# Test-time memory scan of a four-layer transformer: where VectorE forms the second activation and the second scores of a chunk

## What is computed

```python
def step(carry, xs):                       # for every token
    Sm = et * Sm - tt * gt                 # momentum of the gradient
    Wm = (1.0 - at) * Wm + Sm              # memory weights W1, W2 (32x32 each)
    return ((Sm, Wm), Wm)
for c0 in range(0, S, CHUNK):              # CHUNK = 64 tokens
    g = grad(|silu(k W1^T) W2^T - v|^2) at the W of the chunk's start, * 0.1
    g = g * min(1 / max(|g|, 1e-6), 1)     # clipped by its norm, per token
    (S_state, W_state), Wtraj = scan(step, (S_state, W_state), g)
    h = silu(q W1t^T)                      # read-out with the W of each token
    outs.append(h W2t^T)
```

## Time and profile before

| | |
|---|---|
| median of 3 runs | 3209.58 us (3208.36 to 3209.92) |
| profiled execution | 3204.99 us |
| its span | 3203.2 us |
| busy: TensorE, VectorE, ScalarE, GpSimd | 2956.0, 2241.2, 1444.0, 734.6 us |
| the scan (first `hd` to last `retr`) | 2798.90 to 2986.27 us |
| TensorE matmul / VectorE / GpSimd busy from 2799.00 to 2986.30 | 167.04 / 112.60 / 102.36 us |

### The profile page before, as it was taken

The page is one execution under the profiler, slowest core; times in us unless marked ns, Lnnn a source line. Parts: engine busy times, 40 slices in busy tenths (PEclk is TensorE's granted clock), DMA queues, the critical chain, the costliest instruction groups (busy, mean ns, idle before and its releaser), DMA issues. The chain is left out here.

```text
span 3203.2 us, 43118 instructions
## 1 busy us (share of the span) xinstructions
PE 2956.0 (92%) x15784; PEld 1831.3 (57%) x15784; DVE 2241.2 (70%) x4554; ACT 1444.0 (45%) x2691; POOL 734.6 (23%) x608
## 2 busy tenths in 40 slices
PE   5999999999986999999999999999998666789699
PEld 3666666666653555555555555555554342455487
DVE  5788888888616877777777877777764567766554
ACT  2666666666621444444444444444444310322243
POOL 1000000000000344444444444444443000055100
PEclk7999999999976999999999999999999857555598
DMA  4112212120005101111111101111100000000000
GB/s 95 26 32 44 50 26 51 30 46 21 1 8 119 22 19 40 40 40 40 40 40 27 40 19 35 40 40 40 40 1 31 6 7 3 1 1 1 17 1 14
DMA packets 40336, 95.81 MB, mean 30 GB/s; under 512 B 12296, under 2 KB 29374, under 8 KB 30398
## 3 DMA queue, kind: packets, MB, share of 16 engines
q1 hardware_dynamic: 40126, 93.06, 12.9%
HBM read 35.10 MB, written 7.34 MB: 13 GB/s over the span
## 5 line engine op out<-in xcount | busy, mean ns | idle before, releaser
L916 ACT ACTIVATE l1a_PT<-l1a_st 128x512 f32<-128x512 f32 x1024 | 596.5, 598 | 759.8 <-PE l1a_st L832 755.9
L933 DVE TENSOR_REDUCE l1a_m<-l1a_aux 128x1 f32<-128x512 f32 x1024 | 667.7, 685 | 124.9 <-PE l1a_aux L794 123.0
L441 DVE TENSOR_REDUCE l0s_mquad<-l0s_mx 128x1 f32<-128x512 f32 x1024 | 635.6, 684 | 169.6 <-PE l0s_mx L309 169.6
L883 POOL TENSOR_TENSOR l1a_acc<-l1a_acc,l1a_PT 128x1024 f32<-128x1024 f32 x224 | 569.7, 2543 | 680.5 <-ACT l1a_PT L916 680.5
L417 ACT ACTIVATE l0s_PT<-l0s_st 128x512 f32<-128x512 f32 x1024 | 528.6, 602 | 237.0 <-PE l0s_st L325 234.4
L845 PE MATMUL l1a_ov<-l1a_PT,l1a_V 128*64 128x512 f32 x2048 | 495.7, 605 | 0.0
L830 PE MATMUL l1a_st<-l1a_QA,l1a_KA 128*128 128x512 f32 x1024 | 446.9, 436 | 2.3 <-issue 2.3
L325 PE MATMUL l0s_st<-l_QS,l_KS 128*128 128x512 f32 x1024 | 438.1, 431 | 3.7 <-ACT l0s_PT L417 3.6
L309 PE MATMUL l0s_mx<-l_KS,l_QS 120*128 120x512 f32 x1024 | 415.6, 413 | 20.4 <-DMA l_KS<-qk_rows 20.4
L832 PE MATMUL l1a_st<-l1a_QB,l1a_KB 65*128 65x512 f32 x1024 | 405.3, 396 | 0.0
L794 PE MATMUL l1a_aux<-l1a_KA,l1a_QA 128*128 128x512 f32 x1024 | 398.5, 437 | 0.8 <-DVE l1a_lo L945 0.8
(11 more groups left out here) (352 smaller groups left out, 2844.4 us busy)
## 6 DMA issues: line engine op xcount, KB each, us to landing
l1a_KA<-l1a_hi SPq DMA_DIRECT2D x32, 512.0 KB, 8.1
l_QS<-qk_rows SPq DMA_DIRECT2D x64, 192.0 KB
l_KS<-qk_rows SPq DMA_DIRECT2D x64, 192.0 KB
l1a_QA<-l1a_hi SPq DMA_DIRECT2D x16, 512.0 KB, 4.6
l1a_QA<-l1a_lo SPq DMA_DIRECT2D x16, 512.0 KB, 8.7
l1a_QB<-l1a_hi SPq DMA_DIRECT2D x16, 512.0 KB, 4.6
l1a_KB<-l1a_lo SPq DMA_DIRECT2D x16, 512.0 KB, 6.5
qk_rows<-l0s_hi SPq DMA_DIRECT2D x64, 64.0 KB, 6.8
```

What stands on the lines that cost most here:

```text
L441: nc.vector.tensor_reduce(mquad[:, u % 2, tile, g:g + 1], mx[:, n % MX0, :], axis=AX.X, op=ALU.max).then_inc(mx_free[n % MX0], 1)
L883: nc.gpsimd.tensor_tensor(acc[:, h % 2, 1, :], first, PT[:, g % PT_SLOTS, :], ALU.add).then_inc(added_pool, 1)
L916: nc.scalar.activation(PT[:, g % PT_SLOTS, (u % 2) * CW:(u % 2 + 1) * CW], st[:, u % ST1, :], ACT.Exp, scale=1.0 / float(np.sqrt(HD1))).th ...
L933: nc.vector.tensor_reduce(m4[:, b, q, c:c + 1], src, axis=AX.X, op=ALU.max).then_inc(aux_read, 1)
```

## The change

The read-out moves one chunk nearer on all engines. On VectorE `h2` of chunk c-1 no longer stands between the state writes but behind `side`, ahead of `gn`. `m2` is now of chunk c-1, not c-2, and stands behind the `dwe` pair, ahead of the state write. TensorE does `hh` of c-1 and `y2` of c-2 in iteration c, GpSimd `h2a` and `h2c` of c-1, ScalarE `retr` of c-2, so that each of these loops has one iteration less behind the last chunk. Buffers and instructions are the same in number. The last chunk's `h2` and `m2` follow behind VectorE's loop.

```diff
-            for c in range(NCH + 3):
+            for c in range(NCH + 2):
...
-                if 0 <= c - 2 < NCH:
-                    o = c - 2
+                if 0 <= c - 1 < NCH:
+                    o = c - 1
                     pe.wait_ge(s["h2_ready"], o + 1)
...
                     nc.tensor.matmul(hh, hd[:, o % 3, :], h2[:, :], start=True, stop=True).then_inc(s["hh_full"], 1)
-                if 0 <= c - 3:
-                    o = c - 3
+                if 0 <= c - 2:
+                    o = c - 2
                     pe.wait_ge(s["h2s_ready"], 2 * (o + 1))
                     pe.wait_ge(s["m2_ready"], o + 1)
...
-                if c >= 2:
-                    o = c - 2
+                if c >= 1:
+                    o = c - 1
                     pool.wait_ge(s["h2_ready"], o + 1)
...
+                link(nc.vector.tensor_scalar(side[:, :], pn, hn[:, :], EPS3 ** 2 / NORM_SCALE, ALU.mult, ALU.max))
+                if c >= 1:
+                    second_activation(c - 1)
+                dve.wait_ge(s["zn_full"], c + 1)
...
+                    nc.vector.scalar_tensor_tensor(dwe[:, c % 4, i, :], root.broadcast_to([CHUNK, DM]), 1.0 / COEF_UNIT,
+                                                   grad, op0=ALU.min, op1=ALU.mult).then_inc(s[done], 1)
+                if c >= 1:
+                    second_scores(c - 1)
+                new = (c + 1) % 4
+                dve.wait_ge(s["first_full"], c + 1)
...
+            second_activation(NCH - 1)
+            second_scores(NCH - 1)
```

More of the change, by code:

```diff
@@ L2005, in _ @@
                         pe.wait_ge(s["tok_done"], 3 * c)
-                    if c >= 3:
-                        pe.wait_ge(s["m2_ready"], c - 2)
+                    if c >= 2:
+                        pe.wait_ge(s["m2_ready"], c - 1)
                     nc.tensor.transpose(htok, hd[:, c % 3, :], ident[0:DM, 0:DM]).then_inc(s["htok_full"], 1)
@@ L2011, in _ @@
                         pe.wait_ge(s["w2_done"], c)
-                    if c >= 4:
-                        pe.wait_ge(s["y2_read"], c - 3)
+                    if c >= 3:
+                        pe.wait_ge(s["y2_read"], c - 2)
                     nc.tensor.matmul(dh, W2[:, c % 2, :], dp[:, :], start=True, stop=True).then_inc(s["dh_full"], 1)
@@ L2070, in _ @@
                         nc.scalar.activation(tok[:, i, :], htok, ACT.Copy, scale=half[:, i, c:c + 1]).then_inc(s["tok_done"], 1)
-                if 0 <= c - 3:
-                    act.wait_ge(s["y2_full"], c - 2)
-                    nc.scalar.activation(T["retr"][:, at(c - 3)], y2, ACT.Copy).then_inc(s["y2_read"], 1)
+                if 0 <= c - 2:
+                    act.wait_ge(s["y2_full"], c - 1)
+                    nc.scalar.activation(T["retr"][:, at(c - 2)], y2, ACT.Copy).then_inc(s["y2_read"], 1)
         @block.gpsimd
@@ L2078, in _ @@
             pool.wait_ge(s["consts_done"], 1)
-            for c in range(NCH + 2):
+            for c in range(NCH + 1):
                 if c < NCH:
@@ new lines, in second_activation, with second_scores @@
+            def second_activation(o):
+                dve.wait_ge(s["e2_done"], o + 1)
+                if o >= 1:
+                    dve.wait_ge(s["hh_full"], o)
+                    dve.wait_ge(s["h2s_ready"], 2 * o)
+                nc.vector.scalar_tensor_tensor(h2[:, :], e2[:, :], 1.0, y1, op0=ALU.add, op1=ALU.mult
+                                               ).then_inc(s["h2_ready"], 1)
+            def second_scores(o):
+                dve.wait_ge(s["hh_full"], o + 1)
+                if o >= 1:
+                    dve.wait_ge(s["y2_full"], o)
+                nc.vector.scalar_tensor_tensor(m2[:, :], hh, thM[:, o:o + 1], T["C"][0:CHUNK, at(o)],
+                                               op0=ALU.mult, op1=ALU.mult).then_inc(s["m2_ready"], 1)
```

115 lines of the change are left out of this document (46 added, 69 removed).

## The result

The changed kernel takes 3195.41 us (median of 5 runs, 3189.05 to 3198.23) beside 3209.58 us (5 runs, 3204.42 to 3212.07): ratio 0.9957, 95% interval 0.9944 to 0.9970. That is 13.8 us less by the ratio (9.6 to 18.0 by its interval), 14.2 between the medians. The forecast was 11.6 less, 3198.0 us. The direction and the mechanism came as forecast. The profiled execution took 3189.05 us.

A forecast was written before the change was run, and what follows sets the result against it. The scan was taken as a loop of latencies, 5.66 us between state writes, with no engine full. Savings of 9.0 + 2.6 = 11.6 us, all other parts 0, took 3209.6 to 3198.0 us; range 3195.5 to 3203.0.

The forecast's parts named there:

- The gap ahead of `y1`: TensorE between `z` and `pred`: `y1` no longer waits for `h2`, saving 0.32 us in 28 chunks, 9.0 us.
- The end: Behind the last chunk: the last `hh` starts at about 2980.35 instead of 2982.91, saving 2.6 us.
- `h2` in its new place: VectorE between `side` and `gn`: `h2` fits before `gn` starts, cost 0; up to 0.21 a chunk without cover.
- `gn` still idle ahead of it, about 0.1: Sign of a right forecast on VectorE: idle time ahead of `gn` of about 0.1 in place of 0.31 us.
- `hh` behind it: TensorE: `hh` following the moved `h2` starts 0 to 0.09 us later, cost 0.
- `m2` ahead of the state write: VectorE behind the `dwe` pair: `m2` is hidden, cost 0, with 0.02 to 0.18 us to spare.
- The wait for `first_c` shorter but there: Sign of a right forecast: the state write still waits for `first_c`, but for less time.
- Rival A: `h2` and `m2` lengthen on VectorE beside GpSimd: saving only 4.2 to 7.3 us, 3202.3 to 3205.4 us; chance 0.12.
- B: Gap moves to another wait of `y1` or `pred`; only the stage's end gains 2.6 us: 3207.0 us; chance 0.04.
- C: State write, queued behind `m2`, is held by a late `y2`: slower, 3223 us; chance 0.02.
- Rival D: TensorE's granted clock rises in the scan: up to 22 us more gain, 3176 us; chance 0.02.
- half of the spread of the runs: Allowance at the range's lower end, beside 1.7 us of more gain; the lowest run is 1.2 below the median.

The follow-up runs named there:

- `y1` held back: Changed kernel with one more wait ahead of `y1`, for `e1` of the new chunk; 3214.13 us, ratio 1.0023 against the kernel before.
- `h2` twice: Changed kernel with a second `h2` into a spare buffer ahead of `gn`; 3194.38 us, ratio 0.9961 against the kernel before.
- the two edits together: Changed kernel with `ckq` at the start of GpSimd's iteration and `h2` ahead of `side`; 3190.05 us, ratio 0.9956 against the kernel before.
- `ckq` first: Changed kernel with `ckq` at the start of GpSimd's iteration, not behind the base tiles; 3190.51 us, ratio 0.9956 against the kernel before.
- `m2` twice: Changed kernel with a second `m2` into a spare buffer ahead of the state write; 3196.24 us, ratio 0.9972 against the kernel before.
- `h2` moved alone: Kernel before with `h2` ahead of `gn` and all other lags unchanged; 3267.42 us, ratio 1.0186 against the kernel before.

## Why the prediction was right, and where not

- **The gap ahead of `y1`, 28 x 0.32 = 9.0 us: right.** Measured 8.82 (175.04 - 166.22), with `pred` at 1.12 behind `z` and the writes at 5.33. Chunk 3 of the kernel before had shown both numbers. `y1` held back shows that such a gap is paid in full. The missing 0.14 (28 x 0.32 is 8.96) is less than what a few longer chunks hold. In one of them (2844.69 to 2850.19) `h2` starts 0.52 behind `side`, not 0.24, though `side` is all it is shown to wait for.
- **The end, 2.6 us: right.** Measured 2.69. The last `hh` starts 0.51 behind the start of `e2`; it was 2.68. The last `retr` ends 13.25 us earlier in the profile, of which 1.74 lie ahead of the first state write: 11.5, as forecast.
- **`h2` in its new place, 0: right in the sum, wrong in the steps.** "Right: `gn` still idle ahead of it, about 0.1" failed. `h2` started at the expected place (0.24 behind `side`), but I had taken the start of `gn`, 0.48 behind `zn`, for fixed by `zn`. It was 0.40. Two errors of 0.07 to 0.08, both outside my list of costs, cancelled: `gn` earlier, L2180 slower. `h2` twice and the two edits together show it. That they cancelled is luck, and so is the exactness of the forecast period (5.34 for 5.33): without the second error it is 5.27, as `ckq` first shows, and the gain some 2 us larger.
- **`hh` behind it, 0 to 0.09 later: right in effect.** It starts 0.27 behind the start of `h2` (0.35 before to `y1`), and `y2` stayed clear of `first_c`.
- **`m2` ahead of the state write, 0: right.** `m2` back in its old place gives the same 5.33, `m2` twice puts the slack at 0.11. "The wait for `first_c` shorter but there" failed as a sign: the write starts when `first_c` lets it, 0.35 behind its start in both orders, but the profile shows no idle time where the instruction ahead ended only 0.03 before. The distance to the releaser is the sign to look for, not the bracket.
- **Rival A, VectorE beside GpSimd: right in kind, wrong in place.** I had laid on `h2` and `m2`, which kept 0.21 and went from 0.27 to 0.28. The slowdown struck an instruction that the change doesn't move, because it came 0.08 earlier against GpSimd. L2180 has two SBUF inputs, as the row I had quoted, and its price is 0.07 a chunk.
- **Rivals B and C: fell.** No new name stands on the gap. C's mechanism, the write behind an `m2` that waits, needed the pair to be 4 us late. In `h2` moved alone a pair that is late does cost, at `h2`, 2.05 us a chunk.
- **Rival D: fell.** The granted clock of the scan is 0.50 after as before, with TensorE busy for 161.11 of 173.60 us.
- **The range: too narrow below by 0.1 us.** The step that failed is "half of the spread of the runs" as the whole allowance for the stages outside the scan: half of 1.2 is 0.6 us (3198.0 - 1.7 - 0.6 = 3195.7). With the whole 1.2 the median would have lain inside. Those stages gave 1.74 and 2.65 us in the first pair of profiles. Over all profiles the first state write comes between 2801.3 and 2810.0 us, and what follows it takes 214.2 to 217.1. A forecast from one profile to another median must carry that, whatever the change is worth. The size of the sum, 11.6, lies within the interval of 9.6 to 18.0.

## What to carry to other kernels

In a loop of latencies look for the chunk that happens to lack the suspected wait: its distance to the next one is the forecast, measured. Move a consumer nearer only together with all the loops that free its buffers; here the move of `h2` without them lost 60 us, and with them the change gained 13. After a move, check which instructions now start together on VectorE and GpSimd, those too that nobody moved.

## What the runs showed of the hardware

- A small VectorE instruction with both inputs in SBUF (64x1) takes 0.28 in place of 0.21 us when a GpSimd instruction starts 0.03 ahead of it, and 0.21 when that starts 0.10 or 0.11 ahead, although GpSimd's instruction (0.31 long) overlaps it in both cases. The ends fit one reading, that the VectorE instruction ended no earlier than GpSimd's: in the changed kernel both end at 2864.97, with `h2` twice both end at 2887.71 without any delay, and in the earlier trace rows they end at 2813.22 and 2813.20. The square of `dp` (L2158, 32x64, both inputs in SBUF), off the path, takes 0.24 in place of 0.21 where GpSimd's `slope` starts 0.15 ahead of it. The Trainium skill, SBUF — State Buffer, section Who interferes with whom, says that a VectorE instruction with two SBUF inputs contends with a GpSimd one that reads SBUF. The pair above agrees, and so do `h2` and `m2` with their PSUM input, which kept their durations to 0.01 us; the cost was 0.07 us, what was left of GpSimd's instruction beyond the VectorE one's own 0.21, and not its whole length.
- `gn` began 0.48 behind the matmul it waits for when VectorE was idle with its two waits, and 0.40 when another instruction took the first wait and filled the time. Idle time alone did not do it at the first state write, which starts 0.35 behind `first_c` with 0.31 or with 0.03 of it. That two open waits do it is not shown.
- VectorE starts independent instructions closer together than their durations: 0.13 and 0.14 apart under 0.21 and 0.20 (`h2x` to `h2` to `gn`), 0.20 apart under 0.27 (`m2x` to `m2` to the state write). The cost of an insertion is at most the distance of the starts, less what cover is left.
- The waits view names `hd` for the weight load of `pred` in 28 chunks (0.17 each), but `pred` starts 0.34 behind the matmul in front of it and 0.21 behind the end of `hd`, where the handover from `dp` to `dh` takes 0.05 (2862.84 to 2862.89). With `y1` held back `hd` ended 0.84 before `pred` (2886.29 to 2887.13), and the distance to the matmul in front was 0.35 again. It is the matmuls in front, not `hd`, that set the start.
